# Recurrence phase in nine slots a group: output finished between the next group's levels, two delta buffers, value weights centred once, output squared from PSUM

## The reference, cut to what matters

```python
delta = shifted - h                      # the token before, minus this token
x0 = tanh((h + delta * x_proj_mu) @ xl_w1.T) @ xl_w2.T + xl_b2
mus = einsum(tanh(x0), x_out_w) + x_bias # five mixes: r, w, k, v, g
r = (h + delta * r_mu) @ r_w.T           # k, v, g in the same way
w = tanh((h + delta * w_mu) @ w_w1.T) @ w_w2.T + w_b
wd = exp(-exp(w))                        # decay of a token, per key
o_t = einsum('bhk,bhkv->bhv', r_t, S) + sum(r_t * bonus * k_t) * v_t
S = S * w_t[..., None] + k_t[..., None] * v_t[..., None, :]
o = (o - mean) * rsqrt(var + EPS)        # per head, over its 64 values
o = (o * gn_weight + gn_bias) * silu(g)
return o @ o_w.T
```

## Time and profile before

| what | value |
|---|---|
| time, median of 3 runs | 5213.94 us |
| range of the runs | 5213.09 to 5217.08 us |
| span of the profiled execution | 5221.4 us |
| PE / PEld busy | 86% / 67% |
| DVE / ACT / POOL busy | 56% / 37% / 32% |
| granted clock of TensorE, mean over the span | 0.915 |
| the recurrence phase | some 1,930 us of the span |

### The profile page before, as it was taken

The page is one execution under the profiler, slowest core; times in us unless marked ns, Lnnn a source line. Parts: engine busy times, 40 slices in busy tenths (PEclk is TensorE's granted clock), DMA queues, the critical chain, the costliest instruction groups (busy, mean ns, idle before and its releaser), DMA issues. The chain is left out here.

```text
span 5221.4 us, 80698 instructions
## 1 busy us (share of the span) xinstructions
PE 4498.6 (86%) x29148; PEld 3508.9 (67%) x29148; DVE 2948.3 (56%) x5316; ACT 1946.8 (37%) x3621; POOL 1674.6 (32%) x1322
## 2 busy tenths in 40 slices
PE   6606999999999999689998999899996798888885
PEld 6605988988988899355555555555554677777774
DVE  4484343333433443466666666666664477777775
ACT  2203454444444544233333333333332343334331
POOL 1103434444444343322332232222321223333333
PEclk9999999999999999888888888888887899999998
DMA  6622322222232222100000000000000434434432
GB/s 207 224 84 67 50 50 58 44 60 56 44 58 48 50 46 32 31 17 21 17 22 18 17 22 18 21 17 22 17 17 15 131 82 98 94 88 92 98 65 37
DMA packets 246875, 294.28 MB, mean 56 GB/s; under 512 B 19040, under 2 KB 223584, under 8 KB 242400
## 3 DMA queue, kind: packets, MB, share of 16 engines
q0 software_dynamic: 85760, 117.74, 13.1%
q1 hardware_dynamic: 135136, 137.74, 8.3%
q10 hardware_dynamic: 25600, 33.56, 1.9%
HBM read 154.62 MB, written 134.35 MB: 55 GB/s over the span
## 5 line engine op out<-in xcount | busy, mean ns | idle before, releaser
L578 DVE TENSOR_TENSOR e_hTl<-e_hf,e_hTh 128x512 fp32r<-128x512 f32 x512 | 355.1, 694 | 777.0 <-ACT e_hTh L521 773.9
L1015 POOL TENSOR_TENSOR a_mix<-a_tmp,a_h 128x512 f32<-128x512 f32 x320 | 393.3, 1246 | 1102.4 <-DVE a_tmp L1063 910.4
L442 POOL DMA_INDIRECT acc_d<-e_y,e_sids x256 | 402.2, 1571 | 724.0 <-DVE e_y L594 679.2
L520 ACT ACTIVATE e_hf<-ps_heads,e_b 128x512 f32<-128x512 f32 x512 | 352.3, 688 | 648.5 <-PE ps_heads L665 619.3
L665 PE MATMUL ps<-e_w2h,e_hTh 128*128 128x256 f32 x2048 | 587.4, 287 | 0.0
L665 PE MATMUL ps<-e_w2h,e_hTl 128*128 128x256 f32 x2048 | 585.0, 286 | 0.0
L665 PE MATMUL ps<-e_w2l,e_hTh 128*128 128x256 f32 x2048 | 579.3, 283 | 0.0
L665 PE MATMUL ps_heads<-e_xTh,e_w1h 128*128 128x512 f32 x1024 | 420.0, 410 | 41.4 <-ACT e_hTh L521 29.5
L1357 PEld LDWEIGHTS ps_heads<-a_R,a_K 32*128 32x128 f32 x7168 | 272.6, 224 | 259.9 <-issue 258.3
L665 PE MATMUL ps_heads<-e_xTh,e_w1l 128*128 128x512 f32 x1024 | 409.4, 400 | 0.0
L665 PE MATMUL ps_heads<-e_xTl,e_w1h 128*128 128x512 f32 x1024 | 409.1, 399 | 0.0
(11 more groups left out here) (286 smaller groups left out, 10199.1 us busy)
## 6 DMA issues: line engine op xcount, KB each, us to landing
r_x<-in_L_attn_hidden_states SPq DMA_DIRECT2D x32, 512.0 KB
xn_d<-r_xn ACTq DMA_DIRECT2D x32, 512.0 KB, 3.1
xnT_d<-r_xT ACTq DMA_DIRECT2D x32, 512.0 KB, 3.5
acc_d<-r_zeros POOLq DMA_DIRECT2D x16, 1024.0 KB, 21.2
e_w<-in_L_ffn_w SPq DMA_DIRECT2D x16, 1024.0 KB
s_d<-a_s SPq DMA_DIRECT2D x32, 512.0 KB, 2.9
f_a<-acc_d SPq DMA_DIRECT2D x32, 512.0 KB, 3.8
f_x<-s_d SPq DMA_DIRECT2D x32, 512.0 KB, 5.3
```

What stands on the lines that cost most here:

```text
L442: pool.indirect_dma_start(acc_d, bass.IndirectOffsetOnAxis(ap=sids[:, GT * q + t:GT * q + t + 1], axis=0), ys[r][:, t, :], None, compute_o ...
L520: nc.scalar.activation(hf[m % 2][:], ps[2 + m % 2][:], ACT.Gelu, bias=b1s[:, m:m + 1])
L578: nc.vector.tensor_tensor(hT[q % 2][1][:, m, :], hf[m % 2][:], hT[q % 2][0][:, m, :].bitcast(F32), ALU.subtract).then_inc(h_sb, 1)
L1015: nc.gpsimd.tensor_tensor(mix[n][:, m, :].rearrange("p (c t) -> p c t", c=GT), tmp[i % 2][:].rearrange("p (c t) -> p c t", c=GT), h[q % 2] ...
```

## The change

`SLOTS` goes from 11 to 9. Two numbers are added, `LATE = 2` and `FRONT = 7`. In slots 0 and 1 an engine now does the last two pieces (VAL, then both GATES) of the group whose levels it has just begun; in slots 2 to 8 pieces 0 to 6 of the next group. Chunk steps 0 and 1 are in slots 7 and 8, steps 2 to 8 in slots 0 to 6 of the next group, behind that slot's level. So the sum of squares, the power and the product by `rstd` now stand behind levels 0 and 1.

The diagonal (`own_terms`) becomes a use of the two PSUM banks, number 15 (OWN), in the seventh piece. `delta` has two buffers, so that POOL can make it earlier (`ahead`, after slot 7). The gates are multiplied on DVE at the head of level 2 (`gates`). The weights `v_w` are centred over each head's 64 values once, before the first group; outputs, which are sums of values, are then centred too, so DVE takes no mean off any more, and ACT copies the output from PSUM to `oc` and squares it from PSUM.

The diff, cut to its core:

```diff
-        delta = sb("a_delta", [P, KD, GT, P])
+        delta = [sb(f"a_delta{r}", [P, KD, GT, P]) for r in range(2)]
...
-        SLOTS = 11
+        SLOTS = 9
         CHUNK = LEVELS
-        MIX = [3, 4, 5, 6, 8, 9, 12, 13, 15, 16]
-        LOW, X0, X0T, DLOW, DEXP, KEY, REC, VAL, GATES = 0, 1, 2, 7, 10, 11, 14, 17, 19
-        USES = 21
+        LATE = 2
+        FRONT = SLOTS - LATE
+        MIX = [3, 4, 5, 6, 8, 9, 13, 14, 16, 17]
+        LOW, X0, X0T, DLOW, DEXP, KEY, REC, OWN, VAL, GATES = 0, 1, 2, 7, 10, 11, 12, 15, 18, 20
+        USES = 22
...
-        AT = {2: (0, 1), 3: (2, 3), 4: (4, 5), 5: (6,), 6: (7,), 7: (8, 9)}
+        AT = {2: (0, 1), 3: (2, 3), 4: (4, 5), 5: (6, 7), 6: (8, 9)}
...
+                def chunk_at(s):
+                    if s >= CHUNK:
+                        chunk(g, j, q, s - CHUNK, first)
+                    elif not first:
+                        jp, qp = later(j - 1, q, QB - 1)
+                        chunk(g - 1, jp, qp, s + SLOTS - CHUNK, isinstance(j, int) and j == 0 and q == 1)
+
+                def piece_at(s):
+                    if s < LATE:
+                        piece(g, q, FRONT + s, first)
+                    elif left:
+                        piece(g + 1, f1[1], s - LATE, False)
+
                 for s in range(SLOTS):
                     if s < LEVELS:
                         level(g, r, s, first)
...
+                    if s < LATE or s == SLOTS - 1:
+                        piece_at(s)
+                        chunk_at(s)
                     else:
...
+                        chunk_at(s)
+                        piece_at(s)
+                    if left > 1 and s == CHUNK:
+                        ahead(g + 2, f2[0], f2[1])
                     if left > 1 and s == SLOTS - 1:
...
+                        begin(g + 2, f2[1], False)
+
+            ahead(0, 0, 0)
+            begin(0, 0, True)
+            for s in range(FRONT):
                 piece(0, 0, s, True)
...
             dve.wait_ge(w_in, 16 * (LOADS + 1))
+            value = Order(dve, vw_centred)
+            vheads = vw[:].rearrange("p k (h v) -> p (k h) v", v=DV)
+            value.link(nc.vector.tensor_reduce(vmean[:], vheads, AX_X, ALU.add))
+            value.link(nc.vector.tensor_scalar(vmean[:], vmean[:], -1.0 / DV, None, ALU.mult))
+            value.did(nc.vector.tensor_tensor(vheads, vheads, vmean[:].unsqueeze(2).to_broadcast([P, KD * NH, DV]),
+                                              ALU.add))
...
-                if s in (9, 10):
-                    m = s - 9
+            def gates(f, q):
+                for m in range(KD):
                     dve.wait_ge(th_sb, 2 * f + m + 1)
...
+                if lv == LATE:
+                    gates(g, r)
...
-                if u in (0, 1):
-                    o.n = 2 * u
-                    cs = slice(2 * u, 2 * u + 2)
-                    op = ps[5][:].rearrange("p (c h v) -> p c h v", c=2, h=NH)
-                    dve.wait_ge(o_ps, 2 * g + u + 1)
-                    o.link(nc.vector.tensor_reduce(osum[:, cs, :], op, AX_X, ALU.add))
-                    o.link(nc.vector.tensor_scalar(osum[:, cs, :], osum[:, cs, :], 1.0 / DV, None, ALU.mult))
-                    nc.vector.tensor_tensor(oc[:, cs], op, osum[:, cs, :].unsqueeze(3).to_broadcast([P, 2, NH, DV]),
-                                            ALU.subtract).then_inc(centred, 1)
...
-                if u in (1, 2):
-                    v = u - 1
-                    act.wait_ge(centred, 2 * g + v + 1)
+                if u in (0, 1):
+                    cs = slice(2 * u, 2 * u + 2)
+                    act.wait_ge(o_ps, 2 * g + u + 1)
                     if not first:
...
                         act.wait_ge(var_sb, g)
-                    nc.scalar.activation(sq[:, 2 * v:2 * v + 2], oc[:, 2 * v:2 * v + 2], ACT.Square).then_inc(sq_sb, 1)
+                    nc.scalar.copy(oc[:, cs].rearrange("p c h v -> p (c h v)"), ps[5][:])
+                    nc.scalar.activation(sq[:, cs].rearrange("p c h v -> p (c h v)"), ps[5][:], ACT.Square
+                                         ).then_inc(sq_sb, 1)
...
+                if s == 6:
+                    to = room(OWN)
+                    pe.wait_ge(rkb, f + 1)
+                    for c in range(GT):
+                        done = nc.tensor.matmul(to[:, c * NH:(c + 1) * NH], rk2[q % 2][:, c * P:(c + 1) * P], heads[:],
+                                                start=True, stop=True)
+                    done.then_inc(piece_ps, 1)
```

More of the change, by code:

```diff
@@ L848, in recurrence_phase @@
         order = [1, 2, 0, 3, 4]
-        SLOTS = 11
+        SLOTS = 9
         CHUNK = LEVELS
-        MIX = [3, 4, 5, 6, 8, 9, 12, 13, 15, 16]
-        LOW, X0, X0T, DLOW, DEXP, KEY, REC, VAL, GATES = 0, 1, 2, 7, 10, 11, 14, 17, 19
-        USES = 21
-        BY_ACT = [LOW, X0, X0T, DLOW, DEXP, KEY, REC, VAL, VAL + 1]
+        LATE = 2
[3 more added lines that the diff above has]
+        USES = 22
+        BY_ACT = [LOW, X0, X0T, DLOW, DEXP, KEY, REC, OWN, VAL, VAL + 1]
         BY_DVE = MIX + [GATES, GATES + 1]
-        AT = {2: (0, 1), 3: (2, 3), 4: (4, 5), 5: (6,), 6: (7,), 7: (8, 9)}
+        AT = {2: (0, 1), 3: (2, 3), 4: (4, 5), 5: (6, 7), 6: (8, 9)}
         def pairs_ps(half):
@@ L996, in _, with ahead, begin @@
             pool.wait_ge(set_up, 15)
-            def begin(f, j, q, first):
+            def ahead(f, j, q):
                 r = q % 2
                 pool.wait_ge(h_in[r], 32 * (QB // 2 * j + q // 2) + 32)
-                if not first:
-                    emptied(pool, f - 1, MIX[NMM - 1])
-                nc.gpsimd.tensor_tensor(delta[:], h[r][:, :, :, 0:P], h[r][:, :, :, 1:P + 1], ALU.subtract
+                if not (isinstance(j, int) and j == 0 and q < 2):
+                    emptied(pool, f - 2, MIX[NMM - 1])
+                nc.gpsimd.tensor_tensor(delta[r][:], h[r][:, :, :, 0:P], h[r][:, :, :, 1:P + 1], ALU.subtract
                                         ).then_inc(deltas, 1)
+            def begin(f, q, first):
+                pass
             def piece(f, q, s, first):
@@ L1056, in piece @@
                 r = q % 2
+                if s == 5:
+                    dve.wait_ge(piece_ps, USES * f + REC + 1)
+                    emptied(dve, f, KEY)
+                    stt(out=rk2[r][:], in0=K2[r][:], scalar=bonus[:, 0:1], in1=bank(REC)[:], op0=ALU.mult, op1=ALU.mult
+                        ).then_inc(rkb, 1)
                 for i in AT.get(s, ()):
@@ L1144, in chunk @@
                                             ).then_inc(gated, 1)
-            sequence(dve, begin, piece, own_terms, level, chunk)
+            sequence(dve, ahead, begin, piece, level, chunk)
         @block.scalar
@@ L1176, in piece @@
                     nc.scalar.activation(decay0[r][:], dexp[:], ACT.Exp, scale=-1.0).then_inc(decay_sb, 1)
-                if s == 6:
+                if s == 5:
                     ready(REC)
                     act.wait_ge(rkb, f + 1)
-                    nc.scalar.copy(R2[r][:], bank(q, REC)[:]).then_inc(act_out, 1)
-                if s == 8:
+                    nc.scalar.copy(R2[r][:], bank(REC)[:]).then_inc(act_out, 1)
+                if s == 6:
+                    if not first:
+                        act.wait_ge(diag_sb, f)
+                    nc.scalar.copy(own[:].rearrange("p c h -> p (c h)"), ready(OWN)[:, 0:GT * NH]).then_inc(act_out, 1)
+                    emptied(act, f, OWN)
+                    for hd in range(NH):
+                        for c in range(GT):
+                            done = nc.scalar.activation(A2[r][:, hd, c, :], ident[:], ACT.Copy, scale=own[:, c, hd:hd + 1])
+                    done.then_inc(diag_sb, 1)
+                if s == 7:
                     for u in range(2):
@@ L1219, in level, with chunk @@
                 done.then_inc(A_sb, 1)
-            def chunk(g, j, q, u, last, first):
+            def chunk(g, j, q, u, first):
                 r = q % 2
@@ L1313, in piece @@
                     product(to[:], [(kw[:, k, :], mix[2][:, k, :]) for k in range(KD)]).then_inc(piece_ps, 1)
-                for i in AT.get(s, ()):
-                    mixes(i)
-                if s == 6:
-                    to = room(REC)
-                    have_mix(2)
-                    product(to[:], [(rw[:, k, :], mix[0][:, k, :]) for k in range(KD)]).then_inc(piece_ps, 1)
-                if s == 8:
+                if s == 7:
                     for u in range(2):
```

142 lines of the change are left out of this document (54 added, 88 removed).

## The result

The changed kernel takes 5170.33 us (median of 4 runs, 5165.18 to 5179.46), the kernel before 5215.51 us in the same comparison. The ratio is 0.9918 with a 95% interval of 0.9907 to 0.993: faster, by 45 us or 0.8%. The forecast was 147 us. Rival B, "the clock stays down as long as before", had 5176.

The account below looks back on a forecast made before the run. PE bounds the recurrence's second stretch; waits and a low clock bound the first. Groups falling from 58.3 to 53.8 us give 140 us over 31, plus 7 at the start: 147 less, 5067 us, range 4925 to 5180.

Parts of the forecast that it names:

- Rival B: Recurrence: the clock stays down as long as before, through slots 4 and 5; group 57.3 us, kernel 5176 us, chance 0.19.
- the clock term: Steady group: one fall of PE's clock, in slot 2, costing 4.5 us a group, between 0 and 8.
- The walk at the upper clock: One steady group, slot by slot with PE's clock up: durations sum to 49.3 us, against 58.3 before.
- The new waits: PE waits 0.7 us in slot 7 for REC to be emptied, and idles about 1.3 us in slot 2.
- The product by `rstd`: DVE in slot 2: takes 1.2 us instead of 2.91, since the second buffer lets `delta` run in slot 7.
- the power: POOL's power beside DVE's scaling of `K` and `R` in level 1: holds nothing up, 0, at worst 2.7 us a group.
- The mean: Taking the mean off on DVE goes: counted as nothing, because it stood where PE is never idle.
- The start: Group 0's VAL and GATES leave the serial stretch before the first level: 7 us gained, between 0 and 8.
- Rival A: Recurrence: the clock stays up, no 3 us idle time left; group 49.3 us, kernel 4928 us, chance 0.17.
- Rival C: Slower: clock low from level 1, not recovering before slot 6; group 65 us, kernel 5424 us, chance 0.12.

Follow-up runs that it names:

- e13: The changed kernel with only X0T and its two MIX products padded from 32 to 128 rows: 4961.3 us, ratio 0.9507 to the kernel before.
- e9: The changed kernel, without padding, with the mean on DVE again and the value weights not centred: 5167.6 us, ratio 0.9929 to the kernel before.
- e7: e4 with the mean on DVE again and the value weights not centred: 4964.0 us, ratio 0.9519 to the kernel before.
- e1: The changed kernel with the next group's MIX 6 issued between REC and the second MIX, removing PE's slot 7 wait: 5116.3 us, ratio 0.9811 to the kernel before.
- e4: The changed kernel with the front's narrow products padded with zeros to 128 rows and columns, OWN left at 4 columns: 4900.6 us, ratio 0.9396 to the kernel before.
- e10: The changed kernel, without padding, with one delta buffer instead of two: 5161.1 us, ratio 0.99 to the kernel before.
- e14: The kernel before with only the value weights centred, no mean on DVE, ACT copying and squaring output from PSUM: 5185.7 us, ratio 0.9947.

## Why the prediction was wrong, point by point

**The step that failed** is the clock term: "So I expect one fall a group, in slot 2 ... I take 4.5, and 53.8 us a group." There are two falls. A steady group takes 58.0 us, and 48.3 at the upper clock (level 1 at 2216.52 to level 1 at 2264.86, in the interval without a fall), so the clock costs 9.7 us. e13, which has only the short fall, stands at 51.4 and, where even that is missing, at 48.1: 3.3 us for that one, and 58.0 - 51.4 = 6.6 for the one of slot 8. The forecast's own fall came one slot later and cost 3.3 instead of 4.5. The other was not in the sum, and 9.7 lies outside the bounds of "0" and "8" that I gave: I took slots 7 and 8 for dense work because the row for them showed PE never idle. Dense in time is not what decided. Rival B named the reason ("the narrow products are now closer together") but not the place. That its 5176 us is so near is partly luck: its group, 57.3 us, was 0.7 too short, and its sum left out what the end of the phase and the first groups gained.

**The walk at the upper clock** held, slot by slot, against the same group at the upper clock. Slots 7 and 8: 13.5 forecast, 2246.27 to 2260.01 = 13.7 measured. Slot 0: 5.4 and 4.85. Slots 1, 2, 3: 4.8, 4.8, 3.5 and 4.7, 4.2, 3.7. Slots 4, 5, 6: 4.6, 6.3, 6.4 and 4.7, 6.6, 5.9. Sum 49.3 and 48.3. The first interval of the powers is 49.3 by chance: the first power follows a slot 0 that ran at the lower clock, in which the variance comes earlier against level 1.

**The new waits:** REC's was put at 0.7 and is 0.68; the one behind slot 2 at 1.3 and is 0.62.

**The product by `rstd`** takes 1.25 us instead of 2.91, **the power** holds nothing up. Three rows of DVE beside one of POOL:

```profile
2958.29 2.91 POOL L1041 TENSOR_TENSOR a_rstd<-a_vare,a_power 128x16 f32<-128x16 f32 x1 [9.81 <-DVE a_vare L1147]
...
2960.58 0.43 DVE L1116 TENSOR_TENSOR a_K<-a_K,a_decays 128x256 f32<-128x256 f32 x1 [2.38 <-PE ps_heads L1374]
2960.93 0.42 DVE L1118 TENSOR_TENSOR a_R<-a_R,a_decays 128x256 f32<-128x256 f32 x1
...
2963.68 1.27 DVE L1151 TENSOR_TENSOR a_oc<-a_oc,a_rstd 128x1024 f32<-128x1024 f32 x1
```

The first scaling overlaps the power for its full length. It takes 0.43 us, against 0.42 in the earlier trace rows without it, so the term of 0 was right and the other end, 2.7 us, wrong.

**The mean, "I count nothing for it":** right on the kernels as they are (e9), wrong once the clock is up (e7, 1.75 us a group). In the new order DVE's work of slots 7 and 8 has less cover: level 0 stands behind it, and e7's waits for DVE went from 18.2 to 48.2 us.

**The start,** put at 7 us, gave 9.8 (some 1.6 of them lie ahead of the phase's first product). The end of the phase, 7.8 us, was missing from the sum. By these terms the forecast gain should have been larger, not smaller.

**Rival A,** 4928 us, needed the clock up; the Trainium skill (TensorE: Matmul & The Clock Gate, section Why this matters for your kernels) warns of long idle gaps between bursts of matmuls. By that rule this kernel should have kept its clock, and the traces disagree: the longest waits in the steady group are 0.7 us, and e1 has none ahead of its fall. With the narrow products widened the clock stays up in most groups, and the kernel takes 4900.6 us, 27 less than the rival had.

**Rival C,** 5424 us, had the clock low from level 1 to slot 6. It comes back with VAL and GATES in every group, as was argued against it.

**The row I could have read better** is in the earlier trace rows: behind LOW and X0 the clock fell a second time with 0.99 us of idle time. I took that as proof that short idle time suffices, and looked for idle time. e1 and e4 say that, for the new order, the narrow products were the stronger reading.

## What to carry to other kernels

Cost a change at the upper clock, and then look for what the new order puts next to each other on PE: products that fill few rows or columns take no longer than full ones, but here they decided over 10 of 58 us. Where a timeline shows such a cluster ahead of a fall, try padding the operands with zeros; in this kernel that cost at most 0.1 us for a product (OWN) and gave 270 us on top of the reordering's 45, and 112 in the old order. And before a part is judged by undoing it, see whether the loop has long stretches at the lower clock in every group: there two parts measured nothing, while they were worth 63 and 40 us beside the fix.

## What was not expected of the hardware

- The granted clock fell with PE busy for 9.44 of the 9.5 us before (e1).
- Products of 32 rows, 32 output rows or 4 columns take about as long as full ones at the upper clock (LOW 1.90 and 1.96 us, X0 with X0T 2.09 and 1.88, OWN 0.95 and 1.05).
- Time at the lower clock cost 0.47 us for each us: 30 intervals of the changed kernel took 1727 us with 590 at the lower clock, those of e4 1460 with 24.
- Four kernels with different work and different idle time (changed, e9, e10, and in the old order e14) have the same median interval, 58.0 us, three with 20.5 and one with 17.1 us at the lower clock.
